# A decoder layer with CoPE cross attention: the scores one slot later, digits as bytes in their own buffers

## The reference, cut to what matters

```python
def cope(query, attn_logits, pos_emb):
    npos_max = pos_emb.shape[-1]
    gates = jax.nn.sigmoid(attn_logits)
    pos = jnp.flip(jnp.cumsum(jnp.flip(gates, axis=-1), axis=-1), axis=-1)
    pos = jnp.minimum(pos, npos_max - 1)
    ...
    logits_int = jnp.einsum('bhqd,dn->bhqn', query, pos_emb)
    logits_ceil = jnp.take_along_axis(logits_int, pos_ceil, axis=-1)
    logits_floor = jnp.take_along_axis(logits_int, pos_floor, axis=-1)
    w = pos - pos_floor
    return logits_ceil * w + logits_floor * (1.0 - w)
...
logits = jnp.einsum('bhqd,bhkd->bhqk', Q, K) / jnp.sqrt(jnp.asarray(d, Q.dtype))
scores = jax.nn.softmax(logits + cope(Q, logits, pos_emb), axis=-1)
out = jnp.einsum('bhqk,bhkd->bhqd', scores, V)
```

## Time and profile before

| | us |
|---|---|
| median of 3 runs | 14364.57 |
| lowest and highest | 14324.61, 14424.61 |
| profiled execution | 14339.96 |
| its span, first to last instruction | 14338.3 |

### The profile page before, as it was taken

The page is one execution under the profiler, slowest core; times in us unless marked ns, Lnnn a source line. Parts: engine busy times, 40 slices in busy tenths (PEclk is TensorE's granted clock), DMA queues, the critical chain, the costliest instruction groups (busy, mean ns, idle before and its releaser), DMA issues. The chain is left out here.

```text
span 14338.3 us, 175721 instructions
## 1 busy us (share of the span) xinstructions
PE 11781.3 (82%) x56950; PEld 8123.5 (57%) x56950; DVE 7370.4 (51%) x13140; ACT 4442.6 (31%) x7890; POOL 6522.6 (45%) x5384
## 2 busy tenths in 40 slices
PE   8777999966688888888888888888888888888746
PEld 4554333344466666666666666666666666666522
DVE  0112444422466666666666666666656666665543
ACT  0111333311233333333333333333333333333210
POOL 0000000000466666666666666666666666666500
PEclk9888999977788888888888888888888888888766
DMA  3112222211333333333333333333333333333223
GB/s 75 52 44 55 75 76 75 75 59 65 71 77 85 77 79 84 78 81 83 80 80 84 79 80 85 79 80 83 78 83 80 78 85 79 78 86 78 65 71 102
DMA packets 1054792, 1096.90 MB, mean 77 GB/s; under 512 B 738818, under 2 KB 846082, under 8 KB 989202
## 3 DMA queue, kind: packets, MB, share of 16 engines
q1 hardware_dynamic: 981010, 1087.81, 31.1%
q10 hardware_dynamic: 73728, 8.42, 0.4%
HBM read 884.93 MB, written 210.76 MB: 76 GB/s over the span
## 5 line engine op out<-in xcount | busy, mean ns | idle before, releaser
L921 PE MATMUL c_pickps<-c_table,c_hot 128*128 128x112 f32 x16384 | 3467.2, 388 | 557.6 <-DVE c_over L1212 534.6
L921 PEld LDWEIGHTS c_pickps<-c_table,c_hot 128*128 128x128 f32 x16384 | 3297.9, 265 | 662.5 <-DVE c_over L1212 562.4
L1302 POOL TENSOR_TENSOR c_total<-c_total,c_over 128x384 f32<-128x384 f32 (+3 forms) x3584 | 3295.5, 919 | 467.2 <-DVE c_over L1212 187.4
L1189 DVE COPY_PREDICATED c_pickps<-c_upper,c_pickps 128x256 f32<-128x256 uint32 (+1 forms) x1024 | 798.9, 826 | 3349.8 <-PE c_pickps L921 3349.8
L1302 POOL TENSOR_TENSOR c_total<-c_total,c_middle 128x1024 f32<-128x1024 f32 x512 | 1210.6, 2364 | 2848.5 <-DVE c_middle L1203 2848.5
L1269 POOL IOTA c_digitrow<- 1x128 f32 x1 | 0.3, 256 | 3600.7 <-POOLq L65 3600.7
L1054 ACT ACTIVATE c_over<-c_place,c_thresholds 128x384 f32<-128x384 f32 (+3 forms) x3584 | 1589.2, 526 | 0.0
L1037 ACT ACTIVATE c_place<-c_gateps 128x512 f32<-128x512 f32 x1024 | 611.6, 597 | 2673.4 <-PE c_gateps L894 2673.3
L1212 DVE TENSOR_TENSOR c_over<-c_over,c_pickps 128x384 f32<-128x384 f32 (+3 forms) x3584 | 1407.1, 452 | 0.0
L894 PE MATMUL c_gateps<-c_qa,c_ka 128*128 128x512 f32 x2048 | 1105.2, 622 | 65.8 <-ACT c_place L1037 65.1
L960 PEld LDWEIGHTS c_softps<-c_v,c_probs 128*128 128x128 f32 x8192 | 1070.1, 209 | 138.7 <-issue 105.7
(11 more groups left out here) (213 smaller groups left out, 13625.0 us busy)
## 6 DMA issues: line engine op xcount, KB each, us to landing
c_hot<-t_digits SPq DMA_DIRECT2D x512, 1024.0 KB
t_tables<-c_tablesb SPq DMA_DIRECT2D x256, 256.0 KB, 5.8
c_table<-t_tables SPq DMA_DIRECT2D x1024, 56.0 KB, 2.3
a_q<-t_qa SPq DMA_DIRECT2D x64, 512.0 KB
a_k<-t_ka SPq DMA_DIRECT2D x64, 512.0 KB
c_kb<-t_kb SPq DMA_DIRECT2D x256, 128.0 KB, 6.9
t_digits<-c_anchorrows SPq DMA_DIRECT2D x128, 256.0 KB, 2.3
a_q<-t_qa SPq DMA_DIRECT2D x128, 128.0 KB, 2.4
```

What stands on the lines that cost most here:

```text
L921: mm = nc.tensor.matmul(pick_ps[:, h // 4, 0:WIDTH, r * 8:(r + 1) * 8], hot[t % 2][:, h, :], table[s][:, :, :, t * 16 + h].rearrange("p l ...
L1189: ins = nc.vector.copy_predicated(pick_ps[:, :, at:at + width, :], far.unsqueeze(2).to_broadcast([128, 4, width, 32]), pick_ps[:, :, at + ...
L1302: nc.gpsimd.tensor_tensor(a, a, b, ALU.add).then_inc(s_add, 1)
```

## The change

Parts, in the order of the diff:

- The digits are bytes: `anchor_rows`, the DRAM tensor `t_digits` and two new SBUF buffers `digits`, into which `load_hot` now loads. `compare` reads `digits` and writes float32 to `hot`. `load_hot` waits for the comparison that freed its buffer (`s_hot`) and no longer for the selection.
- Loading v is a step of its own, issued after the digits of slot 3.
- `turn_anchor` waits for the fourth step of `near` and no longer for its last; `near` keeps what is left of the rounding in `rounded` (SBUF) and not in `gate_ps`.
- `turn_peak` and `bases` are one matmul each; VectorE adds `start_at` to the peak (behind the maximum) and to the base (ahead of `less`). `keep_base` is gone.
- TensorE's slot: logits of the slot before, gate, values of the slot before that, sums, gate, turned peak, gate, base, gate, next selection. There are four gates in slot 0 and four in slot 1.
- ScalarE: `past` stands ahead of `lift`, `norm` two slots behind.
- VectorE: mux, two products, reciprocal, a bend, maximum, two bends, row maximum, four bends; then `less`, and then the comparison for the slot after next (slots 0 and 1) or `near` (slot 2). In slot 3 the comparison of the next quad's slot 0 stands ahead of `less`, that of its slot 1 behind.

```diff
+        digits = [sb(f"c_digits{x}", [128, 16, 128], U8) for x in range(2)]
...
             def load_hot(i, s, t):
                 x = t % 2
-                after(sp, s_pickps, 4 * i + t - 1)
+                after(sp, s_hot, 4 * i + t - 1)
...
-                sp.dma_start(hot[x][:, :, :], src).then_inc(s_hotload[x], 16)
+                sp.dma_start(digits[x][:, :, :], src).then_inc(s_hotload[x], 16)
...
             def turn_anchor(i):
-                pe.wait_ge(s_near, i + 1)
                 pe.wait_ge(s_anchor, i + 1)
+                pe.wait_ge(s_edge, 4 * i + 6)
...
-                nc.tensor.matmul(soft_ps[:, 0:128], peak[x][:, :], ident[:, :], start=True, stop=False)
-                nc.tensor.matmul(soft_ps[:, 0:128], start_at[x][:, :], ident[:, :], start=False, stop=True).then_inc(s_peakps, 1)
+                nc.tensor.matmul(soft_ps[:, 0:128], peak[x][:, :], ident[:, :], start=True, stop=True).then_inc(s_peakps, 1)
...
-                nc.tensor.matmul(soft_ps[:, 128:256], ident[:, :], start_at[x][:, :], start=True, stop=False)
                 nc.tensor.matmul(soft_ps[:, 128:256], rowmax[x][:, 0:1].to_broadcast([128, 128]), neg_ident[:, :],
-                                 start=False, stop=True).then_inc(s_baseps, 1)
+                                 start=True, stop=True).then_inc(s_baseps, 1)
...
-                    if t == 1 and ahead:
-                        lift(i + 1, 1 - s, 1)
...
-                    if t == 0 and ahead:
-                        lift(i + 1, 1 - s, 0)
...
+                    if t < 2 and ahead:
+                        lift(i + 1, 1 - s, t)
...
-                nc.vector.scalar_tensor_tensor(out=gate_ps[:, :], in0=rounded[:, :], scalar=EIGHTS, in1=gate_ps[:, :],
+                dve.wait_ge(s_anchor, i + 1)
+                nc.vector.scalar_tensor_tensor(out=rounded[:, :], in0=rounded[:, :], scalar=EIGHTS, in1=gate_ps[:, :],
                                                op0=ALU.subtract, op1=ALU.subtract).then_inc(s_edge, 1)
...
-                nc.vector.tensor_scalar(hot[x][:, :, :], hot[x][:, :, :], digit[:, :], None, ALU.is_equal).then_inc(s_hot, 1)
+                nc.vector.tensor_scalar(hot[x][:, :, :], digits[x][:, :, :], digit[:, :], None, ALU.is_equal).then_inc(s_hot, 1)
...
+                dve.wait_ge(s_top, n + 1)
+                nc.vector.tensor_tensor(peak[x][:, :], peak[x][:, :], start_at[x][:, :], ALU.add).then_inc(s_peak, 1)
...
             def less(n, x):
+                dve.wait_ge(s_baseps, n + 1)
+                nc.vector.tensor_tensor(base[x][:, :], soft_ps[:, 128:256], start_at[x][:, :], ALU.add).then_inc(s_base, 1)
...
-    digit_rows, table_rows = scratch("t_digits", [2, 4, 128, 128]), scratch("t_tables", [2, 256, QUAD])
+    digit_rows, table_rows = scratch("t_digits", [2, 4, 128, 128], U8), scratch("t_tables", [2, 256, QUAD])
```

More of the change, by code:

```diff
@@ L917, in pick @@
                 for h in range(16):
-                    if h == 8 and turn is not None:
-                        turn_anchor(turn)
+                    if h == 8:
+                        between()
                     r = h % 4
@@ L972, in step @@
             def step(i, s):
+                ahead = not final(i)
                 for t in range(4):
                     n, x = 4 * i + t, t % 2
-                    behind = not (isinstance(n, int) and n == 0)
-                    ahead = not final(i)
-                    if behind:
+                    one = not (isinstance(n, int) and n < 1)
+                    two = not (isinstance(n, int) and n < 2)
+                    if one:
+                        if t:
+                            logits(i, s, t - 1)
+                        else:
+                            logits(i - 1, 1 - s, 3)
+                    piece(i, t, 0)
+                    if two:
+                        if t < 2:
+                            values(n - 2, x, 1 - s)
+                        elif t == 2:
+                            values(n - 2, x, s, i)
+                        else:
+                            values(n - 2, x, s)
+                    if one:
@@ L991, in step @@
-                    logits(i, s, t)
-                    if ahead:
-                        pieces(i, t, 3)
-                    if behind:
-                        if t == 0:
-                            values(n - 1, 1 - x, 1 - s)
-                        elif t == 1:
-                            values(n - 1, 1 - x, s, i)
-                        else:
-                            values(n - 1, 1 - x, s)
-                    if ahead:
-                        pieces(i, t, 4)
+                    piece(i, t, 3)
@@ L1017, in _ @@
                 tables(1, n)
-            pick(0, 0, 0)
+            pick(0, 0, 0, lambda: None)
             quads(pe, step)
+            logits(last, 1, 3)
+            values(4 * last + 2, 0, 1)
             add_cope(4 * last + 3, 1)
```

136 lines of the change are left out of this document (68 added, 68 removed).

## The result

| | us |
|---|---|
| changed kernel, median of 4 runs | 13656.37 |
| lowest and highest | 13625.31, 13691.15 |
| kernel before in the same session, median of 4 | 14349.14 |
| ratio, with its 95% interval | 0.95 (0.9467 to 0.9533) |
| profiled execution of the changed kernel | 13691.15, span 13689.2 |

It is 5% faster. The forecast was 13450, the median 206 us above it and inside the range. The stretch table of the changed kernel, with the columns of the earlier trace rows: from the first mux to the last, then the four slots of one quad.

What follows compares the result with a forecast made beforehand. TensorE waiting for VectorE, and VectorE for digits, was taken to bound the CoPE attention. 67.0 us a quad plus 3 us for the clock, 70.0 against 77.3, saved 930 us less some 10: 13450 us, range 13240 to 13760.

Steps and rivals of the forecast that it cites:

- First and second slot: CoPE attention slots with four gates each: 16.5 us each at full clock, against 18.13 and 17.51 before.
- the fourth gate's wait: On TensorE in the first two slots, the fourth gate waits for the third's copy, starts at 9.49, ends at 10.36.
- The four-microsecond gap: VectorE's late digits in the fourth slot, 3.99 us in the quad shown, would go with a quarter of the bytes.
- Rival 3: Digits to the comparison are late all the same, a 3 us wait returns: 13870 us, chance 0.07.
- rival 1: VectorE's comparison on bytes runs at one element per cycle, 1.1 us more in the fourth slot: 13680 us, chance 0.13.
- Third and fourth slot: Slots without gates: 17.6 us and 16.4 us at full clock, the fourth if the digits are there.
- 3 us: Clock loss per quad: 1.5 to 2 us a slot, less in the fourth, last two slots at about 0.85 to 0.90.
- 67.0 at full clock: Sum of a quad's four slots at full clock, 16.5+16.5+17.6+16.4 us, before the clock loss.
- The two additions: VectorE's added additions of 128 columns, to peak and base, 0.33 us each; only the first on the path.
- about 1 us a slot: Sign that the forecast is right: TensorE's idle time ahead of the turned peak stays at this size.
- Rival 2: TensorE's clock no longer falls, since no engine wait over 1.7 us is left: 13190 us, chance 0.11.
- Rival 4: Clock stays at the lower level, logits and values leaving little in the array: slower, 14720 us, chance 0.05.

Runs made afterwards that it cites:

- peak on TensorE: Changed kernel with the first value added to the peak by a second matmul on TensorE and VectorE's addition to the peak removed: 13393 us, ratio 0.934.
- early prefix: Changed kernel with the third slot's prefix sums moved ahead of the turned peak, and on VectorE `near` ahead of `less`: 13204 us, ratio 0.921.
- all sums first: Changed kernel with the third slot's prefix sums and `near` moved early, and the sums ahead of values in all four slots: 13772 us, ratio 0.958.

## Why the prediction was right, and what it mis-sized

**First and second slot: right.** 16.61 and 16.59 us against 16.5. Maximum, gates and the fourth gate's wait (0.47) came as reckoned.

**The four-microsecond gap: right.** The waits for digits are gone (7.5 us in the whole run). Rival 3 falls. The comparison on bytes takes 1278 ns in the median, so rival 1 falls as well. Its mean is 1331 because 132 of the 512 take over 1.3 us, and each of these starts while a GpSimd instruction runs.

**Third and fourth slot: the mechanism right, the size off.** The step is "3 us" for the clock: "A quarter of 8 us of doubled work is 1.5 to 2 us a slot, less in the fourth: 3 us." A quad came out at 71.61 us, 4.6 over the 67.0 at full clock; 1.6 us x 128 is 205 us. Of the 4.6 us, on the mean of the stage, 2.1 are in the third slot, 2.3 in the fourth and 0.2 in the first two. The forecast put the doubled work down to logits and values with nothing wide between, which is what the sums show; it did not see the prefix sums, behind the third slot's waits for peak and row maximum. In the quad shown, the third slot is 1.5 us over, as much as the prefix sums' 3.25 for 1.73. The fourth is 2.5 over: the sums' 3.18 for 1.73, the addition's 0.97 for 0.33, and the selection's 6.64 for 6.16. It was not "less in the fourth": there the selection waits for the comparison behind the last product, so a late maximum goes into the slot's length.

**The two additions: one mis-sized.** "I take 0.33 for each." The base's took 0.28, with one operand in PSUM. The peak's took 0.52 in the mean, inside the bounds of 0.25 and 1.13, but for a reason I had not named, and taking it away in the run with the peak on TensorE was worth 263 us. TensorE's idle time ahead of the peak was 642 us, where "about 1 us a slot" makes 512. The excess lay in the forecast's own terms and says nothing of the addition: its third slot alone has 2.2 us of waiting (the sums end at 4.69, the maximum and its addition at 6.80, the turned peak starts 0.1 later), and 2.40 were measured in the quad shown. How the miss divides between the addition and the clock can't be told from these runs, since each moves the other.

**Rival 2** (the clock no longer falls, 13190) fell for this kernel at 0.91, but the early prefix reached 0.96 and 13204. Its premise, "no engine wait over 1.7 us is left", did not agree with those 2.2 us of the third slot, and it was behind that wait that the prefix sums ran slow. **Rival 4** (the clock stays low, 14720) fell too: it needed over 40% of the stage at the lower level, and 0.91 means 18%. In the first two slots there are gates between logits and values, and the clock stays at 1.00, as it does at the fourth slot's sums once a table stands there.

**What was luck.** The 3 us were a guess at a share of doubled work, and the addition's wait for GpSimd was not in the sum at all. That the result lies inside the range owes something to the width given to the range.

Against its own profiled execution the forecast was 13420 and the outcome 13691. Of those 271 us, (7.3 - 5.52) x 128 = 228 are the stage and 56 what the untouched stages happened to take in this execution; the rest is rounding and the end of the stage.

## What to carry to other kernels

Sum a slot at full clock first, then look in the new order for places where TensorE does thin work or waits and a wide product follows: price that product at double, and see whether it can be moved into the wait instead. Look at all slots afterwards: what one slot gains in clock another can lose. Before an addition goes from TensorE to VectorE, look whether both its inputs lie in SBUF and what GpSimd does at that moment. Follow every instruction that stands between the inputs and the result of the critical one on its engine, those of one column too.

## What the runs showed of the hardware

- Matmuls that fill 128 rows and whose result is never read made a kernel 322 us faster; the same with 32 rows made it 234 us slower. The granted clock in the stage was 0.97 with the one and 0.89 with the other.
- In the quads shown, TensorE's waits of 2.40 us (third slot) and 2.03 us (second slot with all sums first) were followed by products at 1.2 GHz, and so were logits and values in a row with no wait at all (fourth slot's sums). Behind waits of 0.79 us with gates around them the clock stayed at 1.00.
- VectorE's addition of two SBUF operands ends 0.15 us after the GpSimd instruction under which it starts (all 219 cases in the changed kernel), and takes 0.3 to 1.1 us; with one operand in PSUM it took 0.27 to 0.29 us in all 512.
- A comparison of 2048 byte elements into float32 takes 1.28 us in the median, as with float32 elements. It has one SBUF input, and the 132 of 512 that took longer (up to 2.11 us) all started while a GpSimd instruction ran.
- Stages with no edit differed by 56 to 60 us between executions, with the granted clock: from 500 to 1000 us it was 0.89 in the execution before and 0.83 in that after.
